# Two heads' transposed probabilities leave PSUM in one instruction per engine

## What is computed

```python
def reference(x, L0_tok_W, L0_tok_b, L0_attn_emb_weight, L0_attn_qkv_w, L0_attn_o_w, L0_ffn_w_gate,
              L0_ffn_w_up, L0_ffn_w_down):
    h = _L0_tok_ref(x, L0_tok_W, L0_tok_b)          # gelu(x[:, 1:] @ W1 + x[:, :1] @ W2 + b)
    h = h + _L0_attn_ref(_layernorm(h, axis=-1), L0_attn_emb_weight, L0_attn_qkv_w, L0_attn_o_w)
    h = h + _L0_ffn_ref(_layernorm(h, axis=-1), L0_ffn_w_gate, L0_ffn_w_up, L0_ffn_w_down)
    return h

# in _L0_attn_ref, with 16 heads of 64:
    scores = jnp.einsum('bhqd,bhkd->bhqk', q, k) * scale + bias
    attn = jax.nn.softmax(scores, axis=-1)
    a = jnp.einsum('bhqk,bhkd->bhqd', attn, v)
    return a.transpose(0, 2, 1, 3).reshape(B, S, N_HEAD * HEAD_DIM) @ o_w.T
```

## Time and profile before

| | us |
|---|---|
| median of 3 runs | 2094.22 |
| lowest and highest run | 2076.9 and 2097.81 |
| span of the profiled execution | 2087.5 |

### The profile page before, as it was taken

The page is one execution under the profiler, slowest core; times in us unless marked ns, Lnnn a source line. Parts: engine busy times, 40 slices in busy tenths (PEclk is TensorE's granted clock), DMA queues, the critical chain, the costliest instruction groups (busy, mean ns, idle before and its releaser), DMA issues.

```text
span 2087.5 us, 46818 instructions
## 1 busy us (share of the span) xinstructions
PE 1901.4 (91%) x15402; PEld 1723.9 (83%) x15402; DVE 1738.7 (83%) x5248; ACT 1463.5 (70%) x4034; POOL 881.6 (42%) x1103
## 2 busy tenths in 40 slices
PE   3799999998999989999999989999999999989995
PEld 1688888888888888888888888888888888878885
DVE  3489899888889879899788888889889788979884
ACT  5477677776777767677676767777677677767773
POOL 0244444444444434444444434434444444444441
PEclk9799999999999999999999999999999999999997
DMA  6000000000000000000000000000000000000000
GB/s 199 29 9 6 15 12 11 15 14 7 14 15 9 14 15 12 9 14 9 14 14 7 14 15 9 14 14 13 8 14 12 12 14 15 6 15 9 6 6 11
DMA packets 24925, 34.92 MB, mean 17 GB/s; under 512 B 2449, under 2 KB 17810, under 8 KB 24674
## 3 DMA queue, kind: packets, MB, share of 16 engines
q1 hardware_dynamic: 15202, 20.03, 3.2%
q10 hardware_dynamic: 8704, 8.36, 1.3%
q0 software_dynamic: 768, 3.21, 0.4%
HBM read 23.17 MB, written 8.42 MB: 15 GB/s over the span
## 4 chain that ended last, share of the span: by engine, by line
PE 54%; DVE 18%; ACT 16%; issue 9%; POOL 0%; DMA 0%; ACTq 0%; DVEq 0%; SPq 0%; POOLq 0%
PE ps L459 30%; PE ps L516 7%; PE ps L527 7%; PE ps L506 7%; ACT prob L699 5%; DVE prob L843 3%; PE ps L469 3%; DVE hT L886 3%; DVE pT L853 3%; DVE gate L877 2%; ACT L699 2%; ACT L675 2%; ACT qk L685 1%; ACT pT L706 1%; DVE heads L862 1%
## 5 line engine op out<-in xcount | busy, mean ns | idle before, releaser
L436 POOL TENSOR_TENSOR prob<-prob,inv 128x510 f32<-128x510 f32 x512 | 529.3, 1037 | 867.0 <-DVE inv L858 866.9
L699 ACT ACTIVATE prob<-prob,neg_top 128x255 f32<-128x255 f32 x1024 | 509.5, 502 | 53.2 <-DVE neg_top L843 52.7
L706 ACT ACTIVATE pT<-ps 128x512 fp32r<-128x512 f32 x512 | 277.9, 595 | 254.4 <-PE ps L516 254.3
L459 PE MATMUL ps<-xnT,wqk 128*128 128x256 f32 x3072 | 424.7, 287 | 1.4 <-DVE xnT L818 1.4
L843 DVE CUSTOM_DVE_ANT_0 prob<-ps,bias 128x255 f32<-128x255 f32 x1024 | 370.6, 418 | 17.6 <-PE ps L506 11.5
L459 PEld LDWEIGHTS ps<-xnT,wqk 128*128 128x128 f32 x3072 | 378.6, 189 | 2.5 <-DVE xnT L818 1.8
L853 DVE TENSOR_TENSOR pT<-ps,pT 128x512 fp32r<-128x512 f32 x512 | 328.3, 682 | 1.6 <-ACT pT L706 1.4
L516 PE MATMUL ps<-ident,prob 128*128 128x128 f32 x2048 | 280.8, 280 | 38.6 <-DVE heads L863 36.7
L527 PE MATMUL ps<-pT,v 128*128 128x256 f32 x2048 | 291.2, 285 | 0.3 <-DVE pT L853 0.3
L516 PEld LDWEIGHTS ps<-ident,prob 128*128 128x128 f32 x2048 | 220.8, 142 | 79.9 <-POOL prob L436 42.1
L527 PEld LDWEIGHTS ps<-pT,v 128*128 128x128 f32 x2048 | 267.9, 189 | 8.0 <-DVE pT L853 0.5
(11 more groups left out here) (89 smaller groups left out, 2645.5 us busy)
## 6 DMA issues: line engine op xcount, KB each, us to landing
xt<-x_cols SPq DMA_DIRECT2D x32, 256.0 KB, 2.6
r_rows<-readout_rows SPq DMA_DIRECT2D x32, 128.0 KB, 3.4
out<-h ACTq DMA_DIRECT2D x32, 128.0 KB
out<-h ACTq DMA_DIRECT2D x32, 127.0 KB
flipped<-bias_rows POOLq DMA_DIRECT2D x1, 3072.0 KB, 17.3
staged<-w_qk SPq DMA_DIRECT2D x8, 256.0 KB, 5.0
staged<-w_v SPq DMA_DIRECT2D x4, 256.0 KB, 8.6
staged<-w_o SPq DMA_DIRECT2D x4, 256.0 KB, 3.2
```

The costliest lines, as they stand in the source:

```text
L436: pool.tensor_tensor(pr, pr, by, ALU.mult).then_inc(prob_done, 1)
L459: mm = pe.matmul(dst, lhs(a, k), rhs(b, k), start=(start and n == 0), stop=(stop and n == last), skip_group_check=skip)
L699: ex = act.activation(pr, pr, ACT.Exp, bias=neg_top[:, g, hh, t:t + 1], scale=-1.0, accum_out=total[:, g, hh, t:t + 1])
L706: act.activation(pT[:, hh, 0].rearrange("p k q -> p (k q)"), ps[:, bank_t[hh], :], ACT.Copy).then_inc(pT_hi, 1)
```

## The change

`probs_hi` and `probs_lo` each become one instruction over both banks, 128 partitions by 1024 columns, where there were two of 512. The ACT instruction waits for the transposes of the second head. `pT_hi` and `pT_lo` count pairs and no longer heads, and PE waits once for the pair before its eight matmuls.

```diff
                 def values_probs(batch, g):
+                    pe.wait_ge(pT_lo, count(PAIRS, batch, g))
                     for hh in range(2):
-                        pe.wait_ge(pT_lo, count(H, batch, 2 * g + hh))
...
                 def probs_hi(batch, g):
-                    for hh in range(2):
-                        act.wait_ge(pT_mm, count(H, batch, 2 * g + hh))
-                        act.activation(pT[:, hh, 0].rearrange("p k q -> p (k q)"), ps[:, bank_t[hh], :],
-                                       ACT.Copy).then_inc(pT_hi, 1)
+
+                    act.wait_ge(pT_mm, count(H, batch, 2 * g + 1))
+                    act.activation(pT[:, :, 0].rearrange("p h k q -> p h (k q)"),
+                                   ps[:, bank_t[0]:bank_t[1] + 1, :], ACT.Copy).then_inc(pT_hi, 1)
...
                 def probs_lo(batch, g):
-                    for hh in range(2):
-                        dve.wait_ge(pT_hi, count(H, batch, 2 * g + hh))
-                        hi, lo = (pT[:, hh, a].rearrange("p k q -> p (k q)") for a in range(2))
-                        dve.tensor_tensor(lo, ps[:, bank_t[hh], :], hi.bitcast(F32), ALU.subtract
-                                          ).then_inc(pT_lo, 1)
+                    dve.wait_ge(pT_hi, count(PAIRS, batch, g))
+                    hi, lo = (pT[:, :, a].rearrange("p h k q -> p h (k q)") for a in range(2))
+                    dve.tensor_tensor(lo, ps[:, bank_t[0]:bank_t[1] + 1, :], hi.bitcast(F32), ALU.subtract
+                                      ).then_inc(pT_lo, 1)
```

## The result

The changed kernel takes 2108.81 us (median of 4 runs, 2108.65 to 2109.78) against 2092.6 us for the kernel before (median of 4). The ratio is 1.0107, with a 95% interval of 1.0072 to 1.0141: slower, by 0.7 to 1.4%. The profiled execution has a span of 2106.8 us, 19.3 us longer than the 2087.5 before. The forecast was 2106.7 us, 12.5 us more than before.

A forecast was written before the change was run, and what follows sets the result against it. PE, busy 91%, bounds the kernel, losing time where it waits for DVE. 0.10 + 0.32 + 0.11 - 0.14 = +0.39 us a batch, 12.5 us over 32, gave 2106.7 us, 0.6% slower; 8-in-10 range 2085 to 2128.

The forecast's parts named there:

- the case in which two banks cost as much as two instructions: Merged instructions take 1.19 us on ACT, 1.36 on DVE: 1.14 us a batch, 36 us, 2131 us; chance 0.09.
- the prediction's second sum: Estimate with 125 ns saved on DVE in place of 0.07 us: 0.17 us less a batch, 7 us slower in all.
- Steps 2 and 3: Late DVE work lengthens PE's wait for the normalised rows, +0.10 us; the late copy delays the exponentials, +0.32 us.
- Step 4: PE's product waits for both heads, 0.28 us later, delaying ACT's `moved`, DVE's `heads_added` and PE's transposes: +0.11 us.
- Steps 5 to 7: DVE leads a `down` product in each of the first two, saving 0.07 us each, -0.14; nothing in the last.
- The wait before step 4's transposes: PE's wait there for `heads_added` on DVE: 1.1 us or so instead of 0.83.
- The total wait for the heads' sum: PE's waits for `heads_added` on DVE before transposes, over the whole run: from 36.7 to some 50 us.
- The wait for the normalised rows: PE's wait for DVE before the layer norm's transposes: growing by 3 us.
- rival B: Slack that looks enough is not: two more places in a batch pay 0.3 us, 19 us, 2126 us; chance 0.19.
- rival A: Saving counts, delay doesn't: 0.07 us of DVE comes off in five places, 11 us faster, 2083 us; chance 0.12.
- ACT's idle time before the copy: ACT waiting for the second head's transposes: growing by about 0.42 us a step, 100 us in all.
- The rival on the other side: The same as rival A: 11 us faster, 2083 us; chance 0.12.

The follow-up runs named there:

- The wait without the merge: Kernel before, all instructions kept at 512 columns, only ACT's first copy also waiting for the second head's transposes; ratio 1.0082.
- the kernel with five steps merged: Changed kernel, but two instructions on both engines in three of a batch's eight steps (1, 3, 4); ratio 0.9942 against the kernel before, median 2069.5 us.

## Why the prediction was right

*The mechanism.* It stood: the saved fixed parts count for little, and the copy that waits for the second head costs in the steps where ACT has no slack. The wait without the merge shows it by itself. The single terms were less good than their sum: some of what follows cancels, and that part of the agreement is luck.

*The instruction sizes.* 1.04 and 1.21 us were forecast by extrapolation, 1.027 and 1.221 measured, so the case in which two banks cost as much as two instructions was out. ACT's copy starts 1.13 us behind the transposes instead of 1.10. In step 1 the remainder starts 2.19 us behind them, 2.18 forecast. What came off is 0.06 us on each engine (1.28 to 1.22 and 1.09 to 1.03), about half of the 125 ns on DVE by which the prediction's second sum went.

*Steps 2 and 3.* +0.10 forecast and +0.07 found; +0.32 forecast and +0.33 found. Step 3 in two instructions took only 0.27 of it back: the 0.06 that DVE's saving brings at the end of step 2 is given back in step 3. The forecast had entered that saving in step 2 and had not asked for it back.

*Step 4.* This term was mis-sized: +0.11 forecast, +0.21 found. The path that was forecast, over ACT's `moved` and DVE's sum, is there when the copy alone is late, with 0.09 us, but another is longer. I had PE's product 0.28 us later, which is right (0.29), but followed only its effect on DVE's sum of the heads and not PE's own queue. Behind the late product stand the feed-forward products, the scores and the next transposes, all on PE, and the wait before those was 0.15 us, less than the delay. Also the first product after a wait for its own weights isn't overlapped, 0.10 us more in the eight. That is 0.29 + 0.10 - 0.15 = 0.24 us, of which 0.21 appears, and with PE's wait by head again in step 4 it falls to 0.08.

*Steps 5 to 7.* -0.14 was forecast for 5 and 6, -0.12 found, as DVE leads there. But step 7, put at nothing, gives 0.06 back: PE arrives earlier there and waits for the remainder of the normalised input. A saving on one engine lasts only until the next place where PE is held by something else.

*The sum.* 0.39 forecast, 0.55 found, 12.5 and 17.6 us over 32 batches. The medians differ by 16.2 us (7 to 14 thousandths by the interval), the traced spans by 19.3. Two terms were left out: the first batch and what follows the last transposes, 2.4 us longer each; and the turns of the loop, with their clock, which can add or take several us. In the two traced runs the clock falls in 9 of 14 turns in both, and a turn differs by 0.1 us at the mean, so they hardly enter there.

*The signs that were named.* The wait before step 4's transposes was put at 1.1 us and is 1.17. The total wait for the heads' sum went to 41.3 us and not to some 50, because it vanished from step 5, where PE now comes later by itself. The wait for the normalised rows fell from 18.6 to 16.9 us instead of growing by 3: the sign was wrongly chosen, since PE itself is late there too. Its values product in step 2 waits for DVE's row maxima (a wait of the weight loads there of 0.15 us in each steady batch, none before), and the product behind it starts 0.14 us later. In the steady batches PE waits for `pT` in steps 4 and 5 and not in 0, 1 or 7, so rival B is out there. At the edges its sign did appear: in the first batch PE waits in steps 1, 3, 4, 5, 6 and 7, and in step 0 behind five of the 14 turns (5.1 us in all), since slack that is enough in the steady state isn't where ACT starts late. That is a few us and not the 19 of the rival. The exponentials of step 3 start 0.34 us later behind the transposes, so rival A's sign is absent. ACT's idle time before the copy grew by 76 us where 100 were forecast.

*The rival on the other side*, that the saving counts and the delay doesn't, is answered by the kernel in which DVE alone is merged: with ACT's delay gone a batch is still 0.17 us longer. PE's wait for the pair in step 4 makes 0.22 of that; the other steps together save only 0.05 us, not the five times 0.07 of the rival, since what steps 2 and 6 save is given back in 3 and 7. The rule of the Trainium skill (Perfetto Trace Analysis, Optimizing Scalar/DVE Operations) that breaking instructions up may let work finish sooner where these engines, not saturated, cause bubbles on others is the one that held for the whole: two instructions in step 3 alone give back 0.27 us. The other, that grouping can help, is stated for an engine that is saturated; DVE at 83% and ACT at 70% are below PE's 91%. Step by step both are seen, as the merged remainder does save 0.06 us in steps 5 and 6, where PE waits for DVE.

## What to carry to other kernels

Before two instructions become one, write down when the first of the two was released and when its first half was used. The merged one starts with the last input and delivers everything with the last output, here 0.44 us later at the start for 0.06 us of fixed cost saved, and only a step with that much slack on both sides can take it. When a late instruction is followed on to what waits for it, follow its own engine's queue as well as the engine that reads its result. And before a total that moved by half a percent is put down to an edit, compare the granted clocks: here the kernel with five steps merged is 0.6% faster, and most of that is a clock that fell in 3 turns instead of 9.

## What the runs showed of the hardware

An ACT copy and a DVE subtraction over two neighbouring PSUM banks cost what the growth with the columns leads one to expect: 1027 ns for 1024 columns against 595 for 512, and 1221 against 682 ns, each within 16 ns of the line through 256 and 512 columns.

Raising a semaphore by 2 behind an ACT or DVE instruction is not free in this program. It brings an instruction of its own (256 more on ACT), the merged copy started 0.06 us later (1.19 instead of 1.13 us behind the transposes), and a batch took 0.15 to 0.18 us more, where DVE's alone made 0.02. The kernels compared also differ in which semaphore the first head uses.

PE's eight products take 1.22 instead of 1.12 us where their first weight load has to wait.

A branch back to the start of the loop costs 2.7 to 6.6 us of the two steps around it (17.0 to 20.9 us against 14.29 in the kernel before), not the same from turn to turn. 2.7 to 2.9 us of it come every time. A stretch of some 3.4 us at 1.2 GHz, with PE standing still no longer than 3 us, adds some 1.5 us (18.5 and 18.75 against 17.1), and a standstill of some 4 us instead of 2.6 another 1.4 (19.9 to 20.2). The kernel before lost the full clock in 9 of 14 turns and the kernel merged in five steps in 3. The place of ACT's loop in its instruction stream shifted ACT's restart from 11.4 to 11.7 us behind the transposes to 8.8 to 10.1. The steady steps repeat to 0.03 us, and the total follows the granted clock, so runs of one kernel differ mostly by their turns; with one trace of each kernel that is argued. The Trainium skill (Runtime: NRT & Kernel Launch, Instruction fetch mechanics) says that instructions are fetched in blocks of 256 and that a taken branch to a place outside the blocks that are loaded forces a fetch before execution goes on. The gaps with "issue" as their releaser agree with that: at every turn on PE (2.4 us in the rows above) and at 12 turns on ACT in the changed kernel (5.9 us there); the size of the blocks no run here shows.
